# A decoder layer on one core: the opening's bias row, weight split and value products are reordered, and the last expert's scatter and stores are done another way

## The chip, the cores and the metric

The kernel runs on one core of one Trainium2 chip, in one launch. The time is device microseconds. The kernel before takes 456.51 us, the median of 3 runs (455.92 to 458.48). The engines have the names of the profile: PE (TensorE matmul) and PEld (its weight loads), DVE (VectorE), ACT (ScalarE), POOL (GpSimd), SP (SyncE, which here only issues DMAs). A name with a q behind it (DVEq, SPq) is that engine's sequencer, the part that fetches instructions, waits on semaphores and hands work to the engine.

## The reference

The input is x of 4 x 128 x 512 and a context of 4 x 2048 x 512 with a bias and a mask for each key. Cut to what matters:

```python
x = x + cross_attention(layernorm(x), ctx, key_bias, mask)   # 16 heads of 32
x = x + self_attention(layernorm(x))                         # 16 heads of 32, clamped
x = x + experts(layernorm(x))                                # 8 experts, 32 rows of each batch

# cross attention
q = tgt @ Wq.T + bq;  k, v = split(ctx @ Wkv.T + bkv)
attn = softmax(q @ (k / sqrt(32)).T + key_bias + pad)
out = attn @ v @ Wout.T + bout

# experts
g, m = top_k(softmax(x @ gate), 32)
h = gelu(x[m] @ w1) @ w2
out = zeros.at[m].add(g * h).astype(bfloat16)
```

The sum of the experts is rounded to bfloat16 and then added to x in fp32.

## The kernel before, in words

The kernel writes out one instruction list for each engine by hand, and semaphores tie the lists together. So the order of the work is the order of the calls in the source, engine by engine. An engine's sequencer takes its list in order. It stops at an instruction whose semaphore is not there yet, and otherwise hands instructions on while the engine is still busy with earlier ones.

Most products are made in three passes: a tensor is split into a rounded part (`*_hi`, made by ACT) and the rest (`*_lo`, made by DVE), and hi x hi, hi x lo and lo x hi are summed in PSUM as fp32r. The scores and the key projection use plain fp32 instead, which the trace shows as two matmul records for each matmul in the source.

**Opening.** SP queues the loads of x, the key weight `wk`, the first context chunk, the query weight `wq`, the value weight `wv`, the self-value weight `sv` and the output weight `wo` (L292 to L297). ACT issues the output bias row `bo_b` by itself (L547), between two of its own casts. PE turns the normed x, projects the keys of the first chunk (`k_block`, L1286), reads two words of a table into registers (`last_chunk`, L269, and `chunk_before_last`, L272), and makes the queries in three rounds of 16 matmuls (`query_terms`, L1440), one for each pair of parts. DVE adds the bias to x (L853), evacuates the keys (L847), makes the low parts of the query weight (L830), of the value weight and of the self-value weight (both L791), and then evacuates the queries (`queries`, L865 and L866). Then it reads the same two words and a third one (L264), and waits for the scores.

**Context chunks.** Only chunks of 128 keys that hold a valid key are visited, 11 here. Chunk t's scores are made by `scores(t)` (L1383 the key bias, L1388 the products). DVE takes the maxima (L892), ACT the exponents (L486), PE turns the probabilities (L1395), DVE copies three of the four banks (L914) and ACT the fourth (L501). PE's `scores(t + 1)` may start only after these four copies, since it writes the same banks. Between these steps PE projects the next chunk's keys (L1286) and values (`v_project`, L1296, four k steps of three matmuls each). In chunk 0 DVE also makes the low part of `wo` in four pieces (`output_split`, L946).

**The end.** After self attention and the routing, the eight experts follow. The last expert's output is made in two halves of 256 columns, `last_out(half, q)`. `last_half` on DVE multiplies a half by its gate (L1254) into `y_s`; ACT rounds it to `y_hi` (L743), DVE makes `y_lo` (L1256), and PE's `last_scatter` adds both to the sum with a 0/1 matrix `back_now` (L1732, L1733). It has one matmul for each batch and part, on a strip of 32 rows of its own. ACT rounds each batch's sum (L746), POOL (half 0) or DVE (half 1, L1267) adds it to x, and SP stores it (L357), eight stores of 128 KB.

## Time and profile before

| | before |
|---|---|
| median of 3 runs | 456.51 us (455.92 to 458.48) |
| the profiled execution's own time | 456.3 us |
| its span, first to last instruction | 454.6 us |
| PE busy | 437.3 us, 96% of the span |
| DVE busy | 367.7 us, 81% |
| ACT busy | 302.4 us, 67% |
| POOL busy | 87.0 us, 19% |
| mean granted clock of PE | 0.994 of full speed |
| mean DMA rate | 180 GB/s |

All times below count from the span's start. PE is busy nearly the whole time, so a change pays where PE waits, or where work behind PE's last matmul gets shorter. Durations of neighbouring instructions overlap a little: four copies of 0.68 us each may start 0.60 us apart. What an instruction costs a full engine is then the distance of the starts.

### The profile page before, as it was taken

The page shows a single profiled execution, that of the slowest core. Times are in us where ns is not written, and L with a number is a line of the kernel's source. Part 1 is how long each engine was busy: PE and PEld are TensorE (multiplying, and loading weights), DVE is VectorE, ACT ScalarE, POOL GpSimd, SP SyncE. Part 2 cuts the span into 40 slices and gives each one's busy share as a digit, 9 for nine tenths or more (in the row PEclk, how much of TensorE's full clock was granted, in tenths as well). Part 3 has the DMA queues.
Part 4 walks back from the last instruction along what each step waited for, and adds up shares of the span by engine and source line. Part 5 has one row for each costly group of instructions (what it writes and reads, how often), then busy time and mean ns, then how long its engine had stood idle before and what let it go on. Part 6 is the DMA issues. An engine that isn't in the chain of part 4 may idle for free.

```text
span 454.6 us, 9856 instructions
## 1 busy us (share of the span) xinstructions
PE 437.3 (96%) x3424; PEld 363.6 (80%) x3424; DVE 367.7 (81%) x516; ACT 302.4 (67%) x623; POOL 87.0 (19%) x111
## 2 busy tenths in 40 slices
PE   8899999999998999999998999999999999999994
PEld 3778888888886779878887787878788787878793
DVE  6888777777778876668888989888989898998862
ACT  4637666666665643667274878778777778787752
POOL 7100000000000122000043240505050321405002
PEclk9999999999999999999989999999999999999999
DMA  8971000000010922700000599999999999897002
GB/s 287 386 263 26 25 23 23 23 23 23 23 26 10 335 85 82 249 32 3 1 0 1 186 387 385 386 386 387 384 323 358 330 331 358 309 370 291 0 1 92
DMA packets 43105, 82.02 MB, mean 180 GB/s; under 512 B 2632, under 2 KB 3784, under 8 KB 43080
## 3 DMA queue, kind: packets, MB, share of 16 engines
q1 hardware_dynamic: 41960, 81.09, 49.6%
q10 hardware_dynamic: 1120, 0.59, 0.5%
q8 instruction: 16, 0.26, 0.2%
q14 instruction: 9, 0.07, 0.0%
HBM read 80.57 MB, written 1.10 MB: 180 GB/s over the span
## 4 chain that ended last, share of the span: by engine, by line
PE 85%; DVE 6%; DMA 4%; ACT 2%; issue 2%; SPq 1%; DVEq 0%; POOL 0%
PE po L1676 18%; PE pk L1676 11%; PE pv L1676 10%; PE pk L1286 8%; PE pv L1296 6%; PE ps L1315 5%; DMA att_w<-in_sv 4%; PE ps L1395 3%; PE pv L1315 3%; PE po L1702 3%; PE ps L1388 2%; PE po L1408 2%; PE po L1315 2%; PE pk L1315 1%; PE ps L1721 1%
## 5 line engine op out<-in xcount | busy, mean ns | idle before, releaser
L1224 DVE TENSOR_TENSOR w_lo<-att_w,w_hi 128x2048 fp32r<-128x2048 f32 x60 | 138.0, 2309 | 21.2 <-ACT w_hi L704 21.2
L704 ACT CAST w_hi<-att_w 128x2048 fp32r<-128x2048 f32 x60 | 115.1, 1918 | 15.5 <-PE po L1676 15.5
L486 ACT ACTIVATE big_a<-ps,negm 128x128 f32<-128x128 f32 x176 | 62.2, 396 | 0.0
L1676 PE MATMUL po<-w_hi,ht_hi 128*128 128x512 f32 (+1 forms) x128 | 50.0, 391 | 0.0
L1676 PE MATMUL po<-w_hi,ht_lo 128*128 128x512 f32 (+1 forms) x128 | 48.7, 380 | 0.0
L1676 PE MATMUL po<-w_lo,ht_hi 128*128 128x512 f32 (+1 forms) x128 | 48.6, 380 | 0.0
L1286 PE MATMUL pk<-ctx_s,att_w 128*128 128x128 f32 x352 | 42.1, 278 | 0.9 <-DMA ctx_s<-in_ctx_t 0.9
L1286 PEld LDWEIGHTS pk<-ctx_s,att_w 128*128 128x128 f32 x352 | 40.2, 192 | 2.8 <-issue 1.8
L486 ACT ACTIVATION_READ_ACCUMULATOR big_a<-ps,negm 128x1 f32 x176 | 41.5, 236 | 0.0
L892 DVE TENSOR_REDUCE mc<-ps 128x8 f32<-128x1024 f32 x22 | 26.9, 1221 | 11.4 <-PE ps L1388 11.3
L1676 PEld LDWEIGHTS po<-w_hi,ht_lo 128*128 128x128 f32 x128 | 24.0, 188 | 5.1
L423 POOL COPY q_now<-qk 128x512 f32 x10 | 6.2, 615 | 113.0 <-PE ps L1388 113.0
L1676 PEld LDWEIGHTS po<-w_lo,ht_hi 128*128 128x128 f32 x128 | 24.1, 188 | 4.4
L1676 PEld LDWEIGHTS po<-w_hi,ht_hi 128*128 128x128 f32 x128 | 24.0, 188 | 4.4
L454 POOL CAST back_now<-state 128x128 fp32r (+1 forms) x8 | 8.6, 1070 | 94.4 <-PE ps L1721 87.5
L1676 PE MATMUL pk<-w_hi,xin_hi 128*128 128x512 f32 x64 | 26.2, 409 | 0.0
L1676 PE MATMUL pv<-w_hi,xin_hi 128*128 128x512 f32 x64 | 25.9, 405 | 0.0
L1676 PE MATMUL pk<-w_hi,xin_lo 128*128 128x512 f32 x64 | 25.3, 395 | 0.0
L1676 PE MATMUL pk<-w_lo,xin_hi 128*128 128x512 f32 x64 | 25.2, 394 | 0.0
L1676 PE MATMUL pv<-w_lo,xin_hi 128*128 128x512 f32 x64 | 25.2, 394 | 0.0
L1676 PE MATMUL pv<-w_hi,xin_lo 128*128 128x512 f32 x64 | 25.2, 394 | 0.0
L1395 PEld LDWEIGHTS ps<-ident,big_a 128*128 128x128 f32 x176 | 21.2, 140 | 4.3
(346 smaller groups left out, 1022.9 us busy)
## 6 DMA issues: line engine op xcount, KB each, us to landing
att_w<-in_w SPq DMA_DIRECT2D x64, 1024.0 KB, 6.9
ctx_s<-in_ctx_t SPq DMA_DIRECT2D x11, 256.0 KB, 2.6
x_s<-in_x SPq DMA_DIRECT2D x4, 256.0 KB, 3.5
att_w<-in_wk SPq DMA_DIRECT2D x1, 1024.0 KB, 8.1
att_w<-in_wq SPq DMA_DIRECT2D x1, 1024.0 KB, 11.3
att_w<-in_wv SPq DMA_DIRECT2D x1, 1024.0 KB, 13.5
att_w<-in_sv SPq DMA_DIRECT2D x1, 1024.0 KB, 16.2
att_w<-in_wo SPq DMA_DIRECT2D x1, 1024.0 KB, 17.2
```

The source lines that it names most:

```text
L486: ins = a.activation(big_a[:, h], ps[:, c, g * P:(g + 1) * P], ACT.Exp, bias=negm[:, h:h + 1], accum_out=sums[:, h:h + 1])
L704: a.copy(w_hi[:, i % SLOTS], att_w[:, i]).then_inc(hi_ok, 1)
L892: v.tensor_reduce(mc[:, hs], ps[:, 2 * half:2 * half + 2].rearrange("p c (g k) -> p (c g) k", k=P), AX.X, ALU.max).then_inc(loop_dve, 1)
L1224: v.tensor_tensor(w_lo[:, i % SLOTS], att_w[:, i], w_hi[:, i % SLOTS], ALU.subtract).then_inc(lo_ok, 1)
L1286: ins = mm(pk[:, g * P:(g + 1) * P], wk_s[:, k, g * P:(g + 1) * P], ctx_s[:, k], start=k == 0, stop=k == KC - 1)
L1296: ins = mm(pv[:], c[:, k], w[:, 1, k], start=k == 0 and c is ctx_hi and w is w_hi, stop=k == KC - 1 and c is ctx_lo, skip_group_check=True)
L1315: ins = mm(dst, l, r, start=n == 0, stop=n == len(pairs) - 1, skip_group_check=True)
L1388: ins = mm(ps[:, c, g * P:(g + 1) * P], q_now[r, g], kt_s[r, g], start=False, stop=True, skip_group_check=True)
L1395: ins = nc.tensor.transpose(ps[:, c, g * P:(g + 1) * P], big_a[:, c * KC + g], ident[:])
L1408: ins = mm(po[c * DH:(c + 1) * DH, 0, g * P:(g + 1) * P], v_s[:, 0, h, 0:DH], big_b[:, h], start=True, stop=True, skip_group_check=True)
L1676: ins = mm(dst, l, r, start=start and i == 0, stop=i == len(terms) - 1, skip_group_check=True)
L1702: ins = nc.tensor.transpose(po[:, 1, c * P:(c + 1) * P], h_s[:, q % 2, c * P:(c + 1) * P], ident[:])
```

## The change

Five places change; nothing else does.

1. The load of `bo_b` is issued by SP behind `wq` and ahead of `wv`, and no more by ACT.
2. DVE evacuates the first keys and splits the query weight first, and adds the bias row to x after that.
3. The self-value weight's low part is no longer made in one piece ahead of the queries. It is made in two pieces of two k steps: one right after the queries, one in chunk 0 between the maxima and the evacuation of the next keys. The pieces of `wo` stay where they were.
4. PE makes two of the first chunk's four value steps ahead of `scores(0)`, and two behind, instead of one and three.
5. In the last half of the last expert, `y_s` is scattered as it is in plain fp32 with the fp32 matrix `back`, without `y_hi` and `y_lo`. Of the last four stores SP issues batches 0 and 2, and ACT batches 1 and 3.

The core of the diff:

```diff
@@ sync
             sp.dma_start(wq_s, wq.rearrange("(k p) n -> p k n", p=P)).then_inc(in_wq, 16)
+            sp.dma_start(bo_b[:], bo.partition_broadcast(P)).then_inc(in_bo, 16)
...
+            for b in range(B):
+                sp.wait_ge(res_pool, b + 1)
+                sp.dma_start(out[b][:, 0:HALF], x_s[:, b, 0:HALF]).then_inc(stored, 16)
+            for n in (0, 2):
+                sp.wait_ge(res_ok, n + 1)
+                sp.dma_start(out[n][:, HALF:D], x_s[:, n, HALF:D]).then_inc(stored, 16)
@@ scalar
             normed_first(2)
-            act.dma_start(bo_b[:], bo.partition_broadcast(P)).then_inc(in_bo, 16)
...
+            def last_halves():
+                act.wait_ge(y_ok, E)
+                act.wait_ge(sc_mm, E - 1)
+                a.copy(y_hi[:, 0:HALF], y_s[:, 0:HALF]).then_inc(y_hi_ok, 1)
+                for b in range(B):
+                    rounding(0, b)
+                for b in range(B):
+                    rounding(1, b)
+                for n in (1, 3):
+                    act.wait_ge(res_ok, n + 1)
+                    act.dma_start(out[n][:, HALF:D], x_s[:, n, HALF:D]).then_inc(stored, 16)
@@ vector
             split_chunk(0)
+            dve.wait_ge(in_cols, 16)
+            k_evacuate(0)
+            query_split(0)
+            query_split(1)
             dve.wait_ge(in_bo, 16)
             for b in range(B):
                 ins = v.tensor_tensor(x_s[:, b], x_s[:, b], bo_b[:], ALU.add)
             link(ins)
-            dve.wait_ge(in_cols, 16)
-            k_evacuate(0)
-            query_split(0)
-            query_split(1)
             split_att(0)
-            split_att(1)
...
+            def part_split(n, first, end):
+                w, slot, _ = SPLITS[n]
+                dve.wait_ge(att_hi_ok, n + 1)
+                ins = v.tensor_tensor(w_lo[:, slot, first:end], w[:, first:end], w_hi[:, slot, first:end], ALU.subtract)
+                if end == KC:
+                    ins.then_inc(att_lo_ok, 1)
+
+            part_split(1, 0, 2)
...
                 moved_maxima(t, nm)
+                if before is None:
+                    part_split(1, 2, 4)
                 k_evacuate(t + 1)
...
                 v.tensor_scalar(y_s[:, cols], (po[:, 0], pk)[half][:, 0:HALF], gcol[:, E - 1:E], None, ALU.mult).then_inc(y_ok, 1)
+                if half:
+                    return
@@ tensor
             v_project(0, 0)
+            v_project(0, 1)
             pe.wait_ge(q_first, 4)
             pe.wait_ge(q_out, 4)
             scores(0)
-            for k in range(1, KC):
+            for k in range(2, KC):
                 v_project(0, k)
...
             def last_scatter(half):
                 cols = slice(half * HALF, (half + 1) * HALF)
+                if half:
+                    pe.wait_ge(y_ok, E + 1)
+                    pe.wait_ge(rounded_ok, B)
+                    for b in range(B):
+                        r = slice(b * CAP, (b + 1) * CAP)
+                        mm(ps[:, b, cols], back[r, E - 1], y_s[r, cols], start=False, stop=False, skip_group_check=True).then_inc(summed_up, 1)
+                    return
```

DVE's list in the opening, from the first chunk's low part to the table reads, before the change. L842 is the chunk's low part, L853 the bias adds, L847 the keys, L830 the query weight's low part, L791 the value and self-value weights', L865 and L866 the queries, L269 a table read:

```order
L842 TENSOR_TENSOR w_lo<-ctx_s,w_hi 128x4x128
L853 TENSOR_TENSOR x_s<-x_s,bo_b 128x512 x4
L847 TENSOR_TENSOR kt_s<-pk,cols 128x512
L830 TENSOR_TENSOR w_lo<-att_w,w_hi 128x4x256 x2
L791 TENSOR_TENSOR w_lo<-att_w,w_hi 128x2048 x2
L865 TENSOR_SCALAR q_now<-ps,cols 128x128
L866 TENSOR_SCALAR qk<-ps,cols 128x4x128
```

The same piece of DVE's list after the change (line numbers moved by a few: L849 is L842, L854 is L847, L837 is L830, L864 is L853, L798 is L791, L871 and L872 are L865 and L866):

```order
L849 TENSOR_TENSOR w_lo<-ctx_s,w_hi 128x4x128
L854 TENSOR_TENSOR kt_s<-pk,cols 128x512
L837 TENSOR_TENSOR w_lo<-att_w,w_hi 128x4x256 x2
L864 TENSOR_TENSOR x_s<-x_s,bo_b 128x512 x4
L798 TENSOR_TENSOR w_lo<-att_w,w_hi 128x2048
L871 TENSOR_SCALAR q_now<-ps,cols 128x128
L872 TENSOR_SCALAR qk<-ps,cols 128x4x128
```

The four adds stand two splits later, and one of the two weight splits ahead of the queries is gone. Where it went, after the last query and in chunk 0 (L884 is the new split, L908 the maximum, L911 its negation, L916 and L918 the moved maxima, L854 the next keys):

```order
L872 TENSOR_SCALAR qk<-ps,cols 128x4x128
L884 TENSOR_TENSOR w_lo<-att_w,w_hi 128x1024
L269 TENSOR_LOAD table
...
L908 TENSOR_REDUCE mc<-ps 128x8
...
L918 TENSOR_TENSOR neg_max<-neg_max,negm 128x16
L884 TENSOR_TENSOR w_lo<-att_w,w_hi 128x1024
L854 TENSOR_TENSOR kt_s<-pk,cols 128x512
```

One half stands between the queries and the table reads, so the reads are further back in the list; the other half stands ahead of the next keys.

PE's list around the first scores, before (L1440 the queries' third round, L1296 one value step in three matmuls, L1383 and L1388 the scores):

```order
L1440 MATMUL ps<-tr_hi,w_lo 128x512 x16
L1296 MATMUL pv<-w_hi 128x512
L1296 MATMUL pv<-w_lo,w_hi 128x512
L1296 MATMUL pv<-w_hi,w_lo 128x512
L1383 MATMUL ps<-bias,ones 128x512 x4
L1388 MATMUL ps<-kt_s,q_now 128x128 x16
```

and after (L1452, L1308, L1395 and L1400 are the same lines):

```order
L1452 MATMUL ps<-tr_hi,w_lo 128x512 x16
L1308 MATMUL pv<-w_hi 128x512
L1308 MATMUL pv<-w_lo,w_hi 128x512
L1308 MATMUL pv<-w_hi,w_lo 128x512
L1308 MATMUL pv<-w_hi 128x512
L1308 MATMUL pv<-w_lo,w_hi 128x512
L1308 MATMUL pv<-w_hi,w_lo 128x512
L1395 MATMUL ps<-bias,ones 128x512 x4
L1400 MATMUL ps<-kt_s,q_now 128x128 x16
```

Three value matmuls moved from behind the scores to ahead of them. At the end of PE's list the eight fp32r matmuls of the second scatter (L1732 and L1733, four each) become these four:

```order
L1744 MATMUL ps<-y_s,state 128x256 x4
```

The matrix is read from `state`, where `back` lives, and no longer from `back_now`.

## Rows read from the trace of the kernel before

**Rows 1.** The page's busy times, with the share of the span.

```profile
PE 437.3 (96%) x3424; PEld 363.6 (80%) x3424; DVE 367.7 (81%) x516; ACT 302.4 (67%) x623; POOL 87.0 (19%) x111
```

**Rows 2.** Chain that ended last, 0 to 42 us: start us, us, what.

```profile
23.24 2.29 DVE w_lo L791
...
28.54 0.67 DVE qk L866
```

**Rows 3.** Timeline of PE: start us, us, engine line op out<-in xcount [idle before <-releaser].

```profile
16.39 3.97 PE L1440 MATMUL ps<-tr_hi,w_hi 128*128 128x512 f32 x16 [0.80 <-ACT w_hi L516]
...
23.94 3.89 PE L1440 MATMUL ps<-tr_hi,w_lo 128*128 128x512 f32 x16
...
28.14 0.39 PE L1296 MATMUL pv<-w_hi,w_lo 128*128 128x512 f32 x1
29.30 0.40 PE L1383 MATMUL ps<-bias,ones 32*128 32x512 bf16 x4 [0.78 <-DVE qk L866]
...
41.13 0.40 PE L1383 MATMUL ps<-bias,ones 32*128 32x512 bf16 x4 [0.16 <-issue]
```

**Rows 4.** Timeline of ACT and its queue in the opening and chunk 0.

```profile
8.41 0.33 ACTq L547 DMA_DIRECT2D bo_b<-in_bo  x1
...
15.20 1.04 ACT L516 CAST w_hi<-att_w 128x1024 fp32r<-128x1024 f32 x1 [1.95 <-DMA att_w<-in_wq]
...
40.31 0.59 ACT L501 COPY big_b<-ps 128x512 f32<-128x512 f32 x1 [1.04 <-PE ps L1395]
```

**Rows 5.** Timeline of the end, from the last half's gate on.

```profile
447.87 0.48 DVE L1254 TENSOR_SCALAR y_s<-pk,gcol 128x256 f32<-128x256 f32 x1 [3.47 <-PE pk L1676]
...
449.64 0.40 PE L1732 MATMUL ps<-y_hi,back_now 32*128 32x256 f32 x4 [1.81 <-issue]
...
450.14 1.20 ACT L746 CAST rounded<-ps 128x256 bf16<-128x256 f32 x4 [1.35 <-PE ps L1733]
450.55 1.43 DVE L1267 TENSOR_TENSOR x_s<-x_s,rounded 128x256 f32<-128x256 f32 x4 [1.01 <-ACT rounded L746]
```

**Rows 6.** The last two stores by line (ns, first and last start us), and landing.

```profile
L357 SPq DMA_DIRECT2D out<-x_s x2: 448/449/450, 451.9 to 452.4; - x2
...
DMA to landing us min/median/max: 1.8/1.8/1.8
```

**Rows 7.** The bias row's DMA: KB, and us from issue to landing.

```profile
bo_b<-in_bo ACTq DMA_DIRECT2D x1, 256.0 KB, 5.8
```

**Rows 8.** DMA queues in 11.7 to 12.7 us: packets, MB, share of 16 engines.

```profile
q1 hardware_dynamic: 137, 0.27, 70.6%
q10 hardware_dynamic: 66, 0.14, 35.9%
```

**Rows 9.** Sequencers' table reads by line: durations ns, first and last start us.

```profile
L272 PEldq SEQ_ASSERT  x1: 18/18/18, 15.9 to 15.9; - x1
...
L269 DVEq TENSOR_LOAD <-table x1: 550/550/550, 27.9 to 27.9; - x1
...
L264 DVEq SEQ_ASSERT  x1: 23/23/23, 30.4 to 30.4; - x1
```

**Rows 10.** Timeline of DVE in the opening and chunk 0.

```profile
14.94 2.48 DVE L853 TENSOR_TENSOR x_s<-x_s,bo_b 128x512 f32<-128x512 f32 x4
...
18.06 2.35 DVE L830 TENSOR_TENSOR w_lo<-att_w,w_hi 128x1024 fp32r<-128x1024 f32 x2
...
30.65 1.23 DVE L892 TENSOR_REDUCE mc<-ps 128x8 f32<-128x1024 f32 x1 [1.45 <-PE ps L1388]
...
36.46 0.69 DVE L847 TENSOR_TENSOR kt_s<-pk,cols 128x512 f32<-128x512 f32 x1 [1.32 <-PE pk L1286]
...
40.10 0.68 DVE L914 COPY big_b<-ps 128x512 f32<-128x512 f32 x1
```

**Rows 11.** The first scores' matmuls by line: durations ns, first and last start us.

```profile
L1388 PE MATMUL ps<-kt_s,q_now x32: 265/270/270, 29.5 to 30.3; 32*128 32x128 f32 x32
```

More of the change, by code:

```diff
@@ L352, in _ @@
                     sp.dma_start(att_w[:, i], w_tile(e, i)).then_inc(raw_in[i], 16)
-            for half in range(2):
-                cols = slice(half * HALF, (half + 1) * HALF)
-                for b in range(B):
-                    sp.wait_ge((res_pool, res_ok)[half], b + 1)
-                    sp.dma_start(out[b][:, cols], x_s[:, b, cols]).then_inc(stored, 16)
+            for b in range(B):
[4 more added lines that the diff above has]
+                sp.dma_start(out[n][:, HALF:D], x_s[:, n, HALF:D]).then_inc(stored, 16)
             sp.wait_ge(stored, 32 * B)
@@ L736, in expert, with rounding @@
                 a.copy(y_hi[:], y_s[:]).then_inc(y_hi_ok, 1)
-            def last_half(half):
+            def rounding(half, b):
                 cols = slice(half * HALF, (half + 1) * HALF)
-                act.wait_ge(y_ok, E + half)
-                if half == 0:
-                    act.wait_ge(sc_mm, E - 1)
-                a.copy(y_hi[:, cols], y_s[:, cols]).then_inc(y_hi_ok, 1)
-                for b in range(B):
-                    act.wait_ge(summed_up, half * B + b + 1)
-                    a.copy(rounded[:, b, cols], ps[:, b, cols]).then_inc(rounded_ok, 1)
+                act.wait_ge(summed_up, half * B + b + 1)
+                a.copy(rounded[:, b, cols], ps[:, b, cols]).then_inc(rounded_ok, 1)
+            def last_halves():
+                act.wait_ge(y_ok, E)
+                act.wait_ge(sc_mm, E - 1)
+                a.copy(y_hi[:, 0:HALF], y_s[:, 0:HALF]).then_inc(y_hi_ok, 1)
+                for b in range(B):
+                    rounding(0, b)
[4 more added lines that the diff above has]
+                    act.dma_start(out[n][:, HALF:D], x_s[:, n, HALF:D]).then_inc(stored, 16)
             expert(0, True)
@@ L751, in _ @@
             expert(E - 1, False)
-            last_half(0)
-            last_half(1)
+            last_halves()
         @block.vector
@@ L940, in attended @@
                 v.tensor_tensor(natural(norm[:, b]), natural(state[:, b]), by_head(norm_c[:, b]), ALU.mult).then_inc(normed[1], 1)
-            def output_split(k):
-                w, slot, _ = SPLITS[2]
-                dve.wait_ge(att_hi_ok, 3)
-                ins = v.tensor_tensor(w_lo[:, slot, k], w[:, k], w_hi[:, slot, k], ALU.subtract)
-                if k == KC - 1:
-                    ins.then_inc(att_lo_ok, 1)
             def chunk(t, before, at_end=False):
@@ L962, in chunk @@
                 else:
-                    output_split(0)
+                    part_split(2, 0, 1)
                 turned_probs(t, 0)
                 if before is None:
-                    output_split(1)
+                    part_split(2, 1, 2)
                 if at_end:
@@ L981, in _ @@
             chunk(0, None)
-            output_split(2)
-            output_split(3)
+            part_split(2, 2, 3)
+            part_split(2, 3, 4)
             with dve.Fori(1, prev) as t:
@@ L1725, in last_scatter @@
                 cols = slice(half * HALF, (half + 1) * HALF)
+                if half:
[5 more added lines that the diff above has]
+                    return
                 pe.wait_ge(back_staged, E)
-                pe.wait_ge(y_lo_ok, E + half)
-                if half:
-                    pe.wait_ge(rounded_ok, B)
+                pe.wait_ge(y_lo_ok, E)
                 for b in range(B):
```

## The prediction

> **What bounds the kernel now.** I read the busy times first: PE works 96% of the span [rows 1]. So the change can pay only where PE waits at the opening, or behind PE's last weight product. The chain of waits comes next. In the opening it runs through the self-value weight: its low part on DVE from 23.24, the queries behind it up to 28.54 + 0.67 = 29.21, and then the first scores [rows 2]. PE's own timeline shows the price: the third value matmul starts at 28.14, and PE could go on 0.23 later, at 28.37. The scores start at 29.30 [rows 3]. That is 0.93 us lost, 0.78 of it shown as idle for the queries. Further back PE waits 0.80 us for the rounded query weight [rows 3], whose cast starts when its load lands, at 15.2 [rows 4]. At the end the stretch behind the last product is serial: gate at 447.87, scatter at 449.64, rounding at 450.14, add at 450.55 [rows 5], last store issued at 452.4 and landed 1.8 later [rows 6].
>
> **Query weight sooner (part 1).** `bo_b` is 256 KB. ACT issues it at 8.41 [rows 4] and it lands 5.8 later [rows 7], at 14.2, ahead of the query weight's 15.2 [rows 4]. In 11.7 to 12.7, when the query weight is arriving, ACT's queue q10 moves 0.14 MB beside 0.27 MB on q1 [rows 8]. All of the bias row thus comes out of the query weight's time: 0.26 MB at the 0.41 MB per us of that window is 0.64 us. Behind it in one queue, the row no longer does this: the weight lands near 14.55, its first half is rounded by 15.6, and PE could start at 15.7 in place of 16.39. But PE also reads its two table words, and the last step of that stands at 15.9 whatever the weight does (it waits for the table, not for the weight) [rows 9]. So PE starts the queries at about 16.05: **0.35 us**, with 0 (the row never was in the way) and 0.67 (the reads don't bind) as ends. `wv`, `sv` and `wo` have the same bytes ahead of them as before.
>
> **DVE's new order (part 2).** The adds of 2.48 us [rows 10] move from ahead of the keys to behind the query weight. Keys, query weight, adds and value weight (0.6 + 2.3 + 2.5 + 2.3) from 15.65 on end at about 23.3. The first query is complete on PE one quarter into the third round, 23.94 + 0.97 = 24.9 less 0.35. So DVE waits for PE there by 1.2 us, and the order costs nothing. The cover is gone only if the bias row lands after about 19.8.
>
> **The self-value split and the value step (parts 3, 4).** Without the second 2.3 us split, each query is evacuated as PE finishes it. PE's last round ends at 27.83 - 0.35 = 27.5, DVE's last query about 1.0 later, 28.5. Two value steps keep PE busy until 28.37 + 0.70 - 0.35 = 28.7, so the first scores start at about 28.75 in place of 29.30 and end at 30.05 in place of 30.59. PE's hole is full, and PE reaches the next keys 1.2 us sooner. What is late next is DVE. Its maximum started at 30.65, right behind the scores [rows 10], but its three table reads had ended only at 30.4 [rows 9]. They began at 27.9, which is when PE's last query came (27.83): DVE's sequencer hangs on that query's semaphore and then runs ahead of its engine. From 27.9 to 30.45 they take 2.6 us. After the change they begin at 27.55 + 0.05, end at 30.2, and the maximum starts at 30.25: **0.40 us** earlier, not 0.55. This needs the sequencer to pass the new half split while two queries are still queued ahead of it. The first read's 27.9 [rows 9] against the last query's start at 28.5 [rows 2] shows it two instructions ahead, not three.
>
> The Trainium skill ("Advanced Engine Details and Errata", section Engine Queue Depths) gives VectorE a queue of 8. By that rule the reads start at once, as I take it; if two were the limit, they would wait for the half split to move up, the case of the first rival.
>
> The first half split, (2.35)/2, about 1.15 us [rows 10], lies between 28.5 and 30.25, and is free. The second lies in the 1.32 us in which DVE waited for the keys [rows 10]. PE now brings these keys early enough, so the wait becomes work and about 0.2 us are left over. DVE is full from there to its third copy, which ended at 40.10 + 0.68 = 40.78 [rows 10]. It now ends 0.40 + 0.20 sooner, 40.2. The second scores stood at 41.13 [rows 3], 0.35 behind that copy, since ACT's copy ended at 40.31 + 0.59 = 40.90 [rows 4]. ACT's chain moves by over 1 us, so some 0.15 of this goes too. I take **0.75 us** for the whole opening. From the second scores on PE runs with hardly a gap, and what it gains there is kept. The ends are -0.15 (the reads wait for the half split) and 1.35 (no table read binds, neither on PE nor on DVE).
>
> **The end (part 5).** Before, PE starts 449.64; now it needs only the gated half, 447.87 + 0.48 = 448.35, and PE starts 0.1 later, at 448.45: 1.19 us sooner. The fp32 scatter is dearer. The first scores are fp32 on the same four strips of 32 rows: 32 records of 128 columns start within 0.8 us [rows 11], 0.028 apart, so the strips run side by side, and each strip takes 0.11 a record. For 256 columns that is 0.22 a record, two records for each batch, and then 0.27 + 0.11 until the second is through: the first batch is ready 0.61 after the start. Before it took 450.14 - 449.64 = 0.50 to ACT's reaction, and would take 0.64 now. So ACT starts at 449.1, **1.05 us** sooner. The ends are 0.5 (strips one after another: the fourth batch comes at 8 x 0.22 + 0.16, 0.55 later than ACT would take it) and 1.2. POOL's adds of half 0 are not on this path. Then the stores: DVE's fourth add ended at 450.55 + 1.43 = 451.98 and the last store was issued at 452.4 [rows 5, 6], because the issues, the last two of 0.45 each, queued on SP. With two on each sequencer the last is issued right behind its add: **0.3 us**, ends 0 and 0.35, landing unchanged. Together 1.35.
>
> On the stores a page of the Trainium skill speaks against hoping for more: "Trainium Kernel Development and Optimization", Key Constraints, says that all queues share the same 16 DMA engines, so that issuing from several saves only issue time. That is the 0.3 above.
>
> **The sum.** 0.75 + 1.35 = 2.1 us. The profiled execution took 456.3 (span 454.6, the other 1.7 unchanged) and would take 454.2. It lies 0.2 under the median of 456.5, so I predict 454.4. A measurement of this kernel can tell about 0.5%, 2.3 us, from no change; the forecast lies just inside this, and its own range is 453.9 to 454.9.
>
> **Rivals.**
> - *The opening gives nothing.* DVE's reads wait until the half split starts (28.4 and not 27.6), the maximum then starts near 31.0, 0.4 later than before. The filled gap gives 0.2 back. Or the query weight is no earlier, since another load takes the bytes. For it: the reads are the last to end already now, 0.2 before the maximum. Against: the sequencer did pass two. Total gain 1.2 to 1.6, 455.1.
> - *The reads don't bind.* They begin 0.6 earlier, or overlap better, and the opening gives what the load and PE's hole offer, 1.35. Total 2.7, 453.8. Against it: both sequencers' reads stand within 0.2 us of what follows them.
> - *The strips are serial in fp32* in the scatter. Total 1.5 to 1.6, 455.0. Against: the 0.028 us spacing [rows 11].
> - *Slower: ACT's stores land late.* The large load from ACT's queue took 5.8 us to land [rows 7], SP's stores 1.8 [rows 6]. If a store from ACT took what its load did, the last would land 4.0 later, and the time would be 456.5 - 2.1 + 4.0 = 458.4. It decides from a landing of 3.9 us on. Against: in the 5.8 us the DMA engines were full with SP's weights; at the end they are empty.
>
> **Chances.** Forecast 0.47, nothing from the opening 0.24, reads don't bind 0.17, serial strips 0.08, slower 0.04 (that the edits don't act as written: none left over, since the order lists show each). Faster by over 0.5% means under 454.2: the 0.17 and somewhat under half of the forecast's 0.47, 0.38 in all. Slower 0.04. Same 0.58. The range runs from the second rival's 453.8 less 0.4 to the first's 455.1 plus 0.7.
>
> **What would show it.** Right: q1 alone active until the query weight has landed near 14.6; PE's queries at 16.05; the first scores at 28.75 with no idle before them; DVE's maximum at 30.2 to 30.3 with the reads just ended; the second scores near 40.35. At the end: PE's scatter 0.58 behind the gate's start, ACT 0.65 behind that, the last store issued within 0.1 of the last add. Wrong: a maximum at or after 30.65, a query start still at 16.4, an ACT store that lands later than SP's, or a gain that is given back in a later chunk.

## Result: 453.72 us against 456.51, and the profile after

| | before | changed |
|---|---|---|
| median (lowest to highest), us | 456.51 (455.92 to 459.11), 7 runs | 453.72 (452.63 to 455.0), 7 runs |
| ratio, 95% interval | | 0.9925 (0.9901 to 0.9948) |
| profiled execution, us (span) | 456.3 (454.6) | 455.0 (453.3) |

The kernel is 0.75% faster. Timed twice more, each time beside the kernel before on one chip, the changed kernel gave 0.9946 (0.993 to 0.9962) and 0.9959 (0.9945 to 0.9973), that is 2.3 and 2.0 us instead of 2.8. The time lies inside the whole range of the prediction (453.4 to 455.8), but 0.7 us under the predicted 454.4 and just outside the 453.9 to 454.9 that the forecast claimed for itself. It is nearest to the second rival's 453.8. "No change beyond 0.5%" was held likelier (0.58) than a faster kernel (0.38), and the first interval lies wholly beyond 0.5%; those of the two repeats reach across it.

The two profiled executions differ by only 1.3 us. Three differences make this up, each read from TensorE's (PE's) and VectorE's (DVE's) timelines:

| stretch, us | before | changed | difference |
|---|---|---|---|
| start to second scores | 41.13 | 39.95 | -1.18 |
| second scores to first expert product | 206.11 | 207.32 | +1.21 |
| first expert product to last half's gate | 200.63 | 200.62 | 0 |
| gate to the end | 6.72 | 5.40 | -1.32 |

**The opening.** PE's timeline of the changed kernel, in the columns of [rows 3]:

```profile
15.77 3.96 PE L1452 MATMUL ps<-tr_hi,w_hi 128*128 128x512 f32 x16 [0.18 <-issue]
...
23.30 3.90 PE L1452 MATMUL ps<-tr_hi,w_lo 128*128 128x512 f32 x16
...
28.17 0.39 PE L1308 MATMUL pv<-w_hi,w_lo 128*128 128x512 f32 x1
28.49 0.40 PE L1395 MATMUL ps<-bias,ones 32*128 32x512 bf16 x4
...
39.95 0.40 PE L1395 MATMUL ps<-bias,ones 32*128 32x512 bf16 x4 [0.47 <-DVE big_b L930]
```

The first scores no longer wait: the value steps end as they start (the 0.78 us of [rows 3] are gone). The query starts 0.62 us sooner, and what released it is no longer ACT's cast but "issue", PE's own sequencer. ACT's timeline shows that the weight was there long before, at 14.20 for 15.20 [rows 4], and the queue of the bias row is now SP's:

```profile
11.33 0.62 ACT L543 CAST w_hi<-ctx_s 128x512 fp32r<-128x512 f32 x1 [0.75 <-DMA ctx_s<-in_ctx_t]
11.86 0.58 ACT L481 CAST tr_hi<-pv 128x512 fp32r<-128x512 f32 x1
12.33 0.59 ACT L481 CAST tr_hi<-ps 128x512 fp32r<-128x512 f32 x1
14.20 1.04 ACT L518 CAST w_hi<-att_w 128x1024 fp32r<-128x1024 f32 x1 [1.28 <-DMA att_w<-in_wq]
```

In 11.7 to 12.7 us one queue is left of the two of [rows 8], and the row now lands 11.7 us after its issue, harmlessly:

```profile
q1 hardware_dynamic: 209, 0.41, 106.2%
```

```profile
bo_b<-in_bo SPq DMA_DIRECT2D x1, 256.0 KB, 11.7
```

The sequencers' reads, answering to [rows 9] (durations in ns, first and last start in us):

```profile
L272 PEldq SEQ_ASSERT  x1: 18/18/18, 15.6 to 15.6; - x1
...
L269 DVEq TENSOR_LOAD <-table x1: 547/547/547, 27.2 to 27.2; - x1
...
L264 DVEq SEQ_ASSERT  x44: 23/23/23, 29.8 to 159.0; - x44
```

PE's reads ended at 15.6, and not at 15.9 as the forecast held fixed. DVE's began at 27.2, while the half split stood at 28.16 in its list; so its sequencer did not wait for the split, which settles the first rival. DVE's timeline, answering to [rows 10]:

```profile
18.57 2.49 DVE L864 TENSOR_TENSOR x_s<-x_s,bo_b 128x512 f32<-128x512 f32 x4
...
24.43 0.35 DVE L871 TENSOR_SCALAR q_now<-ps,cols 128x128 f32<-128x128 f32 x1 [1.04 <-PE ps L1452]
...
28.16 1.22 DVE L884 TENSOR_TENSOR w_lo<-att_w,w_hi 128x1024 fp32r<-128x1024 f32 x1
29.86 1.23 DVE L908 TENSOR_REDUCE mc<-ps 128x8 f32<-128x1024 f32 x1 [0.48 <-PE ps L1400]
...
34.27 1.22 DVE L884 TENSOR_TENSOR w_lo<-att_w,w_hi 128x1024 fp32r<-128x1024 f32 x1
35.40 0.69 DVE L854 TENSOR_TENSOR kt_s<-pk,cols 128x512 f32<-128x512 f32 x1
```

The adds are hidden (DVE still waits 1.04 us for the first query), and the second half split fills what was a wait of 1.32 us for the keys [rows 10]: the keys now follow without a wait.

**The end**, all engines, answering to [rows 5]. The profile shows each fp32 product of the source as two records, so the four are x8 here. The last two rows are the issues of the stores on SP and ACT (start and length of the stretch that holds both):

```profile
447.89 0.48 DVE L1264 TENSOR_SCALAR y_s<-pk,gcol 128x256 f32<-128x256 f32 x1 [3.46 <-PE pk L1689]
...
448.43 0.71 PE L1744 MATMUL ps<-y_s,state 32*128 32x256 f32 x8 [0.58 <-DVE y_s L1264]
449.16 1.20 ACT L742 CAST rounded<-ps 128x256 bf16<-128x256 f32 x4 [1.69 <-PE ps L1744]
449.56 1.43 DVE L1279 TENSOR_TENSOR x_s<-x_s,rounded 128x256 f32<-128x256 f32 x4 [1.19 <-ACT rounded L742]
450.02 1.00 SPq L359 DMA_DIRECT2D out<-x_s  x2
450.36 1.01 ACTq L754 DMA_DIRECT2D out<-x_s  x2
```

The gate stands where it stood, and every later step 1.0 to 1.4 us earlier. ACT's two stores, by line:

```profile
L754 ACTq DMA_DIRECT2D out<-x_s x2: 344/353/362, 450.4 to 451.0; - x2
...
DMA to landing us min/median/max: 1.8/1.8/1.9
```

The last is issued at 451.0 (452.4 in [rows 6]) and lands as fast as one of SP's: the slower rival is out.

**The routing took it back in this one execution.** Stretches of 4 us; the columns are length, PE, PEld, DVE, ACT and POOL busy (with counts), PE's granted clock (1.00 is 2.4 GHz, 0.50 is 1.2 GHz), DMA share, GB/s. Before:

```profile
232.00:236.00 4.00, 4.00 (x24) 3.60 (x24) 3.20 (x18) 3.38 (x7) 1.48 (x4) 0.76 0.00 0
236.00:240.00 4.00, 3.58 (x13) 2.29 (x11) 2.84 (x14) 2.19 (x2) 3.77 (x3) 0.81 0.00 0
240.00:244.00 4.00, 2.63 (x16) 2.11 (x17) 3.15 (x9) 0.44 (x3) 1.47 (x2) 1.00 0.02 4
```

Changed:

```profile
232.00:236.00 4.00, 3.45 (x21) 2.67 (x21) 2.87 (x17) 3.54 (x6) 1.77 (x3) 1.00 0.00 0
236.00:240.00 4.00, 1.90 (x9) 1.27 (x8) 3.69 (x14) 1.00 (x1) 2.73 (x3) 1.00 0.00 0
240.00:244.00 4.00, 3.71 (x17) 3.23 (x17) 2.02 (x6) 0.92 (x3) 2.44 (x2) 0.63 0.02 4
244.00:248.00 4.00, 4.00 (x31) 3.92 (x31) 3.13 (x9) 2.78 (x10) 0.00 (x0) 0.95 0.00 0
```

In both PE's clock is at half for a while. Before, this falls on filling products (`keep_busy`, which only fill PE's idle time; nobody needs their result), and behind them PE still waits 1.50 us for DVE's `kt_s`. In the changed kernel's profiled execution it falls on the 32 gather products, all of which the experts wait for: they take 5.30 us from the first start to the last instead of 3.82.

### The profile page after: what moved, and what is told of

Its sections match the earlier page's. It is cut to its first block, busy times and chain, and to the rows that moved or that the text cites. A ratio compares the mean times of both kernels' runs of the same rounds, so it can differ in the third digit from the quotient of the medians.

```text
span 453.3 us, 9856 instructions
## 1 busy us (share of the span) xinstructions
PE 437.7 (97%) x3424; PEld 363.9 (80%) x3424; DVE 367.4 (81%) x516; ACT 302.1 (67%) x622; POOL 86.9 (19%) x111
## 4 chain that ended last, share of the span: by engine, by line
PE 84%; DVE 9%; ACT 2%; issue 2%; DMA 1%; POOL 1%; DVEq 1%; SPq 0%; POOLq 0%
PE po L1689 18%; PE pk L1689 11%; PE pv L1689 10%; PE pk L1298 8%; PE pv L1308 5%; PE ps L1327 5%; PE po L1715 3%; PE ps L1407 3%; PE pv L1327 3%; PE ps L1452 3%; PE ps L1400 2%; PE po L1420 2%; PE pk L1327 1%; PE po L1327 1%; DMA x_s<-in_x 1%
## 5 line engine op out<-in xcount | busy, mean ns | idle before, releaser
L908 DVE TENSOR_REDUCE mc<-ps 128x8 f32<-128x1024 f32 x22 | 26.9, 1221 | 10.4 <-PE ps L1400 10.3
```

The source lines that it names most:

```text
L908: v.tensor_reduce(mc[:, hs], ps[:, 2 * half:2 * half + 2].rearrange("p c (g k) -> p (c g) k", k=P), AX.X, ALU.max).then_inc(loop_dve, 1)
```

## Experiments

All medians stand beside the kernel before on the same chip. There it took 456.07 (e1 to e4), 456.33 (e7, e8, e10, e12), 456.53 (e6, e9, e11, e14), 455.78 (e15, e16) and 456.51 us (e17, e18). "Reads" are the table reads; "the chunk's cast" is ACT's cast of the first context chunk (L543), which starts when the chunk has landed.

### The two halves of the change

**e1_opening**: the changed kernel with the old end (scatter, rounding and stores; the diff is cut to its core).

```diff
-            last_halves()
+            last_half(0)
+            last_half(1)
...
```

> The changed kernel with the last half's scatter and stores as they were before (y_hi and y_lo, eight matmuls, all stores from SP). Theory (the opening is worth about 1.2 us to the second scores, the end 1.3, and the rest of what single executions differ by is the clock in the routing): second scores start near 39.95 against 41.13 before; from the last half's gate to the end of the span 6.7 us as before; median 1.2 us (0.26%) under the kernel before. Rival (my prediction's sizes, and more than 1.3 from the end): second scores near 40.4, median 0.7 under before.

455.40 us, ratio 0.9989 (0.9977 to 1.0): 0.67 us under before by the medians. The interval reaches 1.0, so the times alone don't tell this gain from none. In its profile the second scores stand at 40.10, near my 39.95, but the median is that of the rival.

**e2_end**: the kernel before with the new end (the same edit the other way round).

> The kernel before with the end of the change alone (fp32 scatter of the last half, last four stores from two queues). Theory: second scores at 41.1 as before; from the last half's gate to the end of the span 5.4 us against 6.7; median 1.3 us (0.28%) under the kernel before. Rival (the medians' 2.8 us come mostly from the end): more than 2 us under before.

454.72 us, ratio 0.9974 (0.9964 to 0.9985): 1.35 us under before; gate to end 5.40 us. So by the medians opening and end add up: 0.67 + 1.35 = 2.0, near the two repeats of the whole change (2.3 and 2.0).

### Parts of the opening

**e3_row**: before, with only the bias row moved behind the query weight. **e4_no_row**: changed, with the row back on ACT.

```diff
             sp.dma_start(wq_s, wq.rearrange("(k p) n -> p k n", p=P)).then_inc(in_wq, 16)
+            sp.dma_start(bo_b[:], bo.partition_broadcast(P)).then_inc(in_bo, 16)
...
-            act.dma_start(bo_b[:], bo.partition_broadcast(P)).then_inc(in_bo, 16)
```

> The kernel before with one edit: SP issues the output bias row behind the query weight, ACT no more. DVE's and PE's lists are as before. Theory: the row took its bytes out of the query weight and of the context chunk ahead of it, so the first cast of the query weight starts about 1 us sooner (14.2 against 15.2), the chunk's cast 0.3 sooner, PE's two table reads end 0.3 sooner (15.6) and the queries start at 15.8. The second scores hardly gain (0 to 0.3 us), since DVE's whole self-value split still ends at 25.5 or so ahead of the queries. Rival (the reads end at 15.9 whatever lands when): queries start at 16.05. Second rival (the row in front of wv delays the self-value weight, and DVE's queries get later): second scores later than 41.2.

> The changed kernel with the output bias row issued by ACT at its old place. Theory: queries on PE start at 16.4 as before, all behind 0.6 later than in the changed kernel, the second scores at 40.5 to 40.6, so the row is worth half of the opening's gain. Rival (DVE bounds chunk 0 whatever PE does, so the row is worth nothing there): second scores at 39.95 as in the changed kernel.

e3 456.27 us, 1.0008 (0.9992 to 1.0025); e4 453.89 us, 0.9947 (0.9929 to 0.9966). The row took what the forecast charged to it: from the chunk's cast to the first cast of the query weight it is 3.3 to 3.5 us in the three profiles with the row on ACT (before, e2, e4) and 2.7 to 2.9 in the twelve with it on SP and that cast at its old place. Yet e4 starts the query only 0.07 later than the changed kernel, measured from the chunk's cast (4.51 for 4.44), and its second scores come only 0.06 later (28.68 for 28.62). e4's query stands 1.19 us behind the weight's cast, as in the kernel before; the changed kernel's stands 1.57 behind, so there something other than the weight holds PE. Of my two expectations for e4 the rival was the nearer. And e3 gains nothing in its time: its first scores start 13.11 us behind the query's start, 12.91 before. What is late there is the self-value split, which still stands ahead of DVE's queries and waits for its weight's cast:

```profile
22.65 2.29 DVE L791 TENSOR_TENSOR w_lo<-att_w,w_hi 128x2048 fp32r<-128x2048 f32 x1 [0.39 <-ACT w_hi L476]
```

**e7_split_whole**: changed, with the self-value split in one piece ahead of the queries again. **e8_value_behind**: changed, with the second value step behind the scores again.

```diff
             split_att(0)
+            split_att(1)
...
-            part_split(1, 0, 2)
...
-                if before is None:
-                    part_split(1, 2, 4)
```

```diff
             v_project(0, 0)
-            v_project(0, 1)
...
-            for k in range(2, KC):
+            for k in range(1, KC):
```

> The changed kernel with the self-value split back in one piece ahead of the queries; two value steps still stand ahead of the first scores. Theory (this split is what held the queries): the first scores start at about 29.3, their maximum at 30.65, the second scores at 40.7 to 41.0, so 0.8 to 1.0 us behind the changed kernel there. Rival (the earlier query weight and the value step are the gain): second scores at 39.9 to 40.2.

> The changed kernel with the second value step back behind the first scores. Theory (DVE bounds chunk 0, and it waits first for the first scores): the scores start 0.3 us sooner than in the changed kernel, at 28.2 to 28.3, DVE's maximum stays near 29.8 since its table reads end there, and the second scores stand at 39.9 as in the changed kernel: the value step moved ahead is worth nothing. Rival (PE bounds chunk 0): second scores 0.3 us later or more.

e7 454.49 us, 0.997 (0.9951 to 0.9989); e8 453.91 us, 0.9951 (0.9933 to 0.9968). My expectation for e7 was too large. Its first scores come 0.54 later against the query's start (13.26 us for 12.72), but from the maximum to the second scores it then needs 9.70 us where the changed kernel needs 10.09. DVE does the same work on either side of the maximum, and only 0.13 us are left at the second scores, measured from the chunk's cast (28.75 for 28.62). e7's median stands 0.6 us above e8's of the same comparison; the two intervals overlap, so the times don't settle it. e8's second scores come 0.12 later; its time is that of the changed kernel. The same stretch lies between 28.58 and 28.73 in the eight profiles with the changed opening as it is, so 0.06, 0.13 and 0.12 are hardly more than their scatter. Taken out one by one, row, split and value step thus cost 0.31 us together, where the whole opening gave 0.6 to 0.8. The new place of the bias adds (part 2) was not taken out alone, so what the rest hangs on is not shown.

### What holds the query's start

In all 14 profiles with ACT's casts and PE's reads in their old order, the reads end 4.24 to 4.27 us behind the chunk's cast, wherever that lies (10.83 to 11.71 us). ACT's rows above show why: the casts of turned batches 2 and 3 stand behind the chunk's cast on ACT's list, DVE's remainders of them ahead of the table on DVE's, and the table ahead of the reads.

**e14_cast_later** (run again as **e17_cast_again** beside **e18_changed_again**, the changed kernel itself):

```diff
             transposed(0, 1)
-            split_chunk(0)
             transposed(0, 2)
             transposed(0, 3)
+            split_chunk(0)
```

> The changed kernel with ScalarE's cast of the first context chunk moved behind the casts of the last two turned self-state batches. In nine profiles so far TensorE's table reads ended 4.24 to 4.27 us after that cast began, and the query's first product began 0.16 us after the reads. Theory A (the reads are late because the table stands on VectorE behind the splits of batches 2 and 3, whose casts stand behind the chunk's landing on ScalarE): the reads end 0.4 to 1.0 us sooner against the chunk's cast (less than 3.9 us after the chunk's cast would have begun), and the query starts only 0.2 to 0.4 us sooner, since its weight's cast is next. Rival B (the reads are bound by something else of the opening, such as the key's products ahead of them on TensorE's list): the reads end as before against the landing and the query's start moves later by 0 to 0.3 us, for the chunk's cast comes later. Median by A 453.3 to 453.9, by B 453.7 to 454.2.

**e6_pe_reads_late**: changed, PE's reads behind the first scores and value steps. The wait for the table itself (`table_ok`) stays ahead of the queries.

```diff
-            last = last_chunk(pe)
-            prev = chunk_before_last(pe)
...
+            pe.wait_ge(table_ok, 3)
...
             for k in range(2, KC):
                 v_project(0, k)
+            last = last_chunk(pe)
+            prev = chunk_before_last(pe)
```

> The changed kernel with TensorE's two table reads moved from ahead of the query projection to behind the first batch's scores and value steps. Theory A (the reads bind the query's start in the changed kernel): the first query product no longer stands 0.16 us behind a read but starts when its rounded weight is there, 0.2 to 0.9 us sooner against the chunk's cast (4.4 us after it in the changed kernel, 3.5 to 4.2 here), while the reads cost about their own 0.7 to 1.0 us later only if TensorE doesn't wait there anyway. Rival B (the weight's cast or the turned remainders bind just as well): the start moves by less than 0.1 us. In both cases VectorE's own reads still stand ahead of its first maximum, so the second scores come at most 0.3 us sooner: median 453.4 to 454.0.

e14: 452.97 us, 0.9934 (0.9914 to 0.9953). Its reads and the start of its query, from the rows of line 272 and PE's timeline:

```profile
L272 PEldq SEQ_ASSERT  x1: 18/18/18, 14.6 to 14.6; - x1
```

```profile
15.20 1.17 PE L1452 MATMUL ps<-tr_hi,w_hi 128*128 128x512 f32 x4
```

The chunk's cast now waits for the two ahead of it and not for the landing, so it is no mark here; the query weight's first cast is one (14.01, and 14.20 in the changed kernel). The reads end 0.56 us behind that cast for 1.40, and the query starts 1.19 behind it for 1.57, as in the kernel before (16.39 - 15.20 = 1.19): it is bound by the weight again. That the reads end so much sooner with one cast moved shows the chain.

e6: 453.86 us, 0.9935 (0.991 to 0.996); the query starts at 14.92, 1.27 us behind its weight's cast, and 0.03 behind the start of the last key product (14.89), so here PE is simply full. Its reads, now beside DVE's maximum, cost nothing: from the chunk's cast to the second scores it is 28.19 us for 28.62, so the gain at the query's start is kept. With both, the rival that something other than the table's reads holds the changed kernel's query falls.

> The version with ScalarE's cast of the first chunk behind the casts of the turned batches once more, on one chip with the changed kernel. Theory A (the table's reads bound the changed kernel's query start by 0.35 to 0.4 us and the second scores by as much): the median stands 0.4 to 0.8 us below the changed kernel's of this same comparison, and the second scores come 28.0 to 28.1 us behind the chunk's landing or 0.5 us sooner than in the changed kernel. Rival B (what is gained in the opening is lost in the scatter between executions, since landings and the place of the half clock move the time by 0.5 to 1.5 us): the two medians lie within 0.3 us of each other.

> The changed kernel word for word, as the other side of that comparison: 453.4 to 454.2 us median. A third profiled execution of it: by the theory that the place and length of TensorE's half clock belong to the execution, its routing (second scores to first expert product) is either 205.8 to 206.1 us or 206.6 to 207.8 us, and its time goes with it; the query's first product stands 0.16 to 0.18 us behind TensorE's last table read in any case.

On one chip: e17 453.71 us, 0.9944 (0.9928 to 0.996); e18, the changed kernel, 454.50 us, 0.9959 (0.9945 to 0.9973). The later cast is 0.8 us better by the medians. By the profiles its query starts 1.19 us behind the weight's cast for 1.72, and its second scores come 0.9 us sooner (0.23 of it because the weight came sooner too). The two intervals overlap, so by time alone it isn't settled; the profiles agree in both pairs, with 0.4 to 0.5 us at the query's start. e14's median is the lowest of the study, but its ratio is not clear of the changed kernel's. The changed kernel's own median here is above the 453.4 to 454.2 that I expected.

### What holds DVE's first maximum

**e16_both**: e14, and DVE's two reads ahead of its four query steps (e14's edit is left out of the diff).

```diff
+            last = last_chunk(dve)
+            prev = chunk_before_last(dve)
             queries(0)
...
             part_split(1, 0, 2)
-            last = last_chunk(dve)
-            prev = chunk_before_last(dve)
```

> The changed kernel with two edits together, as a version that may beat both: ScalarE's cast of the first chunk behind the casts of the turned batches (452.97 us median by itself), and VectorE's two table reads moved from behind its four query steps to ahead of them, where it waits for TensorE's first query sum (1.04 us in the changed kernel, 0.81 with the cast moved). Theory A (VectorE's reads, which end 0.04 us ahead of its first maximum, bind that maximum): the maximum begins sooner against the first scores, 1.0 to 1.25 us behind their start where it is 1.38 now, and everything behind comes 0.1 to 0.4 us sooner; median 452.5 to 452.9. Rival B (the scores and the batch's sum bind it as well, and the reads that stood beside the queries' arithmetic now push those later, since 2.6 us of reads don't fit into a wait of 0.8 us where the list stands still): the first query step comes 0.5 to 1.8 us later, the first scores with it, median 453.5 to 454.8.

453.44 us, 0.9947 (0.9928 to 0.9966): no better than e14. DVE's last read now begins at 27.0 and ends at 27.57, 2.05 us ahead of the maximum:

```profile
L264 DVEq TENSOR_LOAD <-table x44: 301/304/320, 27.0 to 158.1; - x44
```

```profile
29.62 1.22 DVE L909 TENSOR_REDUCE mc<-ps 128x8 f32<-128x1024 f32 x1 [0.50 <-PE ps L1401]
```

Still the maximum starts 1.36 us behind the first scores (28.26), as in every kernel of the study but e8 (1.35 to 1.38, while the reads ended 0.04 to 2.05 us ahead of it). The scores bind it, too. That the reads end 0.04 us before it in the changed kernel is a near tie. In e8, whose scores start sooner behind the query (12.59 us for 12.72), the reads do bind: the maximum starts 1.50 us behind the scores and 0.05 behind the reads. Neither side of my expectation came true: nothing gained, nothing lost.

### The stores

**e9_stores_sp**: changed, all four last stores on SP.

```diff
-            for n in (0, 2):
+            for n in range(B):
...
-                for n in (1, 3):
-                    act.wait_ge(res_ok, n + 1)
-                    act.dma_start(out[n][:, HALF:D], x_s[:, n, HALF:D]).then_inc(stored, 16)
```

> The changed kernel with all four of the last stores issued by SyncE, none by ScalarE. The profile of the changed kernel has SyncE's issues 0.67 us apart (450.02 and 450.69) and ScalarE's at 450.36 and 451.03. Theory A (two issuers relieve SyncE's list by what was forecast, 0.3 us): with four issues on one list the last one comes 0.2 to 0.6 us later and the stretch from the last gate product to the end goes from 5.40 to 5.6 to 6.0 us. Rival B (the issues are not the bound, the sums that come 0.33 us apart are): the stretch stays within 0.1 us of 5.40. Median by A 453.9 to 454.4, by B 453.5 to 453.9.

453.87 us, 0.9949 (0.993 to 0.9968), within the scatter; the profile tells more:

```profile
L359 SPq DMA_DIRECT2D out<-x_s x4: 333/437/445, 449.9 to 451.2; - x4
```

With four on one list an issue takes 0.44 us (median) instead of 0.33, while DVE's adds, which they wait for, start 0.33 to 0.35 apart. Gate to end is 5.69 us for 5.40: the second issuer is worth 0.29 us.

### The half clock in the routing

**e12_busy2**, **e11_busy14**, **e10_busy18**: the changed kernel with 2, 14 or 18 filling products ahead of the slots' transposes instead of 10. **e15_again**: the changed kernel word for word.

```diff
-            keep_busy(10, 7)
+            keep_busy(14, 7)
```

> The changed kernel with 2 and not 10 of the idle-filling matmuls ahead of the slots' transpose. Theory: PE is idle for longer ahead of the gathers, the clock is at half in them more often and perhaps for longer: 5.3 us for the gathers in the profile, and a median 0.5 to 1.5 us over the changed kernel's. Rival: no difference.

> The changed kernel with 14 filling products ahead of the slots' transposes instead of 10. TensorE's granted clock was at half once in the routing of every kernel profiled, in the gathers (at 241 to 242 us, 5.3 us for the gathers) or ahead of them (at 232 to 235 us, gathers 3.8 us). Theory A (where the half clock falls is the chip's, not set by these products): the executions fall into two groups 1.2 to 1.5 us apart as they do for the changed kernel, median 453.5 to 454.3, and the profile shows either place. Rival B (more filling keeps the clock up through the gathers): no execution in the upper group, gathers 3.8 us, median 453.2 to 453.7.

> The changed kernel with 18 and not 10 of the idle-filling matmuls ahead of the slots' transpose in the routing. Theory (in some executions PE's clock falls to half while the gathers run, since PE was idle for 2 us just ahead, and this costs about 1.5 us): with the hole filled the gathers run at full clock in every execution, 3.8 us from first to last record against 5.3, the runs of one kernel spread less, and the median is 0.3 to 1 us under the changed kernel's. If the clock falls earlier, among the filling matmuls, the longer row of them delays the transpose by up to 1.5 us instead. Rival (the clock in the routing is no matter of the matmuls there, or the spread has another source): median and spread as in the changed kernel, 453.7, 452.6 to 455.0.

> The changed kernel once more, word for word, for a second profiled execution of the same program beside the first (455.0 us, gathers at half clock, 5.30 us, first expert product 207.32 us behind the second scores). Theory A (where TensorE's half clock falls differs from one execution of one kernel to the next and makes the two groups of times): the profiled execution lies either near 453.7 with gathers of 3.8 us and 205.8 to 206.1 us from the second scores to the first expert product, or near 455.0 with 5.3 and 207.3; a time of 453.4 to 453.9 together with gathers of 5.3 us, or of 455 together with gathers of 3.8 us, would speak against it. Rival B (the place of the half clock belongs to the program's own arrangement): the profile shows gathers of 5.3 us again whatever its time is. Median 453.4 to 454.3 by both.

| kernel | median, us | profiled, us | where at half clock, from | gathers, us | second scores to experts, us |
|---|---|---|---|---|---|
| changed | 453.72 | 455.0 | gathers, 241.0 | 5.30 | 207.32 |
| e15 | 453.47 | 454.55 | ahead, long, 231.3 | 3.82 | 207.21 |
| e18 | 454.50 | 454.93 | ahead, long, 232.5 | 3.80 | 206.83 |
| e12 (2) | 455.09 | 454.35 | ahead and into the gathers, longest, 233.3 | 4.95 | 207.16 |
| e11 (14) | 454.25 | 455.14 | gathers, 241.8 | 5.31 | 207.35 |
| e10 (18) | 453.60 | 455.05 | ahead, long, 231.8 | 3.82 | 207.78 |
| e14 | 452.97 | 452.93 | ahead, short, 232.6 | 3.81 | 205.79 |

The stretches of e15 (first) and e14 (second), in the columns given above:

```profile
228.00:232.00 4.00, 4.00 (x36) 3.97 (x34) 3.72 (x14) 3.19 (x7) 0.74 (x3) 0.91 0.00 0
232.00:236.00 4.00, 4.00 (x14) 3.32 (x14) 1.85 (x11) 2.70 (x6) 1.20 (x3) 0.50 0.00 0
236.00:240.00 4.00, 3.59 (x12) 2.52 (x10) 3.12 (x15) 1.55 (x1) 3.30 (x3) 0.74 0.00 0
240.00:244.00 4.00, 3.06 (x20) 2.54 (x21) 3.01 (x8) 0.87 (x4) 1.89 (x2) 1.00 0.02 4
```

```profile
228.00:232.00 4.00, 4.00 (x39) 3.97 (x37) 3.72 (x16) 3.40 (x7) 0.95 (x3) 1.00 0.00 0
232.00:236.00 4.00, 4.00 (x14) 2.96 (x14) 2.63 (x15) 3.53 (x6) 2.15 (x4) 0.58 0.00 0
236.00:240.00 4.00, 2.76 (x12) 1.74 (x10) 3.69 (x15) 0.40 (x1) 2.13 (x2) 0.99 0.00 0
```

The same program fell to half clock in the gathers once and ahead of them twice, so the place belongs to the execution. That refutes the reading that the change pushed the gathers into half clock. But the other theory's simple link (gathers at full clock, so a time near 453.7) failed too: e15's profiled 454.55 had gathers of 3.82 us and, ahead of them, 6.8 us at half clock where e14 had 3.4. In all 18 profiles the same holds: with one short stretch ahead of the gathers the routing takes 205.8 to 206.2 us, with a long one or with one in the gathers 206.6 to 207.8. The runs of some kernels fall apart by as much: those of e14 into seven at 452.8 to 453.1 and two at 454.5 to 454.6. Those of e11 and e18 spread without such a gap, and the runs without a profile show only a mean clock, so that the half clock makes the groups is likely, not shown. More filling products (14, 18) buy nothing that can be told from the changed kernel. With 2 the median is 1.5 us above that of 18 beside it (455.09 and 453.60), and the clock stayed at half longest. What sets the place isn't settled.

## Why the prediction was near, and where it failed

**The end: right.** Forecast 1.35 us, measured 1.32 in the profile and 1.35 in e2's median (ratio 0.9974, so 0.7 to 1.6 us by its interval). Term by term: PE's scatter at 448.43 for a forecast 448.45; ACT at 449.16 for 449.1 (strips side by side, 8 records in 0.71 us: the serial rival is out); the issuers 0.29 (e9) for 0.3. ACT's stores landed like SP's.

**The opening: the mechanisms mostly right, the start mis-sized.** Forecast 0.75 us at the second scores, measured 1.18 in the profile. The step that failed is "the last step of that stands at 15.9 whatever the weight does (it waits for the table, not for the weight)". True, it waits for the table. But the table waits, over DVE and ACT, for the landing of the first context chunk, and that came 0.34 us sooner. So the query started 0.62 sooner and not 0.35. Of the 0.43 us by which the opening beat its forecast in this profile, 0.27 are this step, and 0.12 more came by the maximum.

Whether the bias row had held up the chunk is not shown. The chunk's cast starts at 11.54 to 11.71 in the three profiles with the row on ACT and at 10.83 to 11.65, 11.25 on average, in the twelve with it on SP where the cast waits for the landing. But e3, whose profile has the chunk's cast at 11.20 and the second scores at 40.45, gained nothing in its median, and its interval leaves at most 0.4 us. So the earlier landing may be luck of the profiled execution.

With the landing taken off, the size was right: measured from the chunk's cast, the opening gave 29.46 - 28.62 = 0.84 us, or 0.62 with e2 (29.24), whose opening is that of before: on both sides of the 0.75. The e1 median says 0.67. The part behind the maximum was right as well: from there to the second scores 10.48 us became 10.09, 0.39 for a forecast 0.35. The row's own 0.35 was too much: with e4 it is 0.07 at the query's start and 0.06 at the second scores, since PE's reads hold the query once the weight is early. The forecast had a reading wrong here. "Both sequencers' reads stand within 0.2 us of what follows them" was so on DVE (0.19), but PE's reads ended at 15.92, 0.47 ahead of the query's 16.39.

**The maximum: right for a wrong reason.** "DVE's three table reads bind it, 0.40, not 0.55" gave 30.25; it came at 29.86. With the 0.27 of the query's start taken off, 0.12 are left. The reads did begin with PE's last query (27.2), with three instructions of the engine still ahead of them, so two are not the limit. The Trainium skill's queue of 8 (Advanced Engine Details and Errata, section Engine Queue Depths) fits this; no run here fills the queue beyond three. But e16 shows that the scores bind just as well. So the rival "the reads don't bind" was half right on DVE: they tie with the scores, and taking them away alone (e16) gave nothing. On PE they did bind, by 0.4 to 0.5 us, which e14 and e6 took away. That the first median, 453.72, lies at this rival's 453.8 is chance: its opening of 1.35 needed both reads not to bind.

**The sum.** Forecast 2.1 us. Measured 2.8, 2.3 and 2.0 in three comparisons, and 2.0 as the sum of the two halves. The size was right within the scatter between comparisons; the first happened to lie at its upper end. What was off is the weight of "same": a gain of 2.1 was set against a bound of 2.3 us, which is nearly an even chance and was given 0.38. The forecast also took no account of the half clock: its place and length made routings of 205.8 to 207.8 us in the profiles, and the changed kernel's profiled executions lie 0.4 to 1.3 us above their medians.

## What to carry to other kernels

Follow a wait that "stands whatever else does" one engine further: here a table of two words on one engine's list hung, through in-order lists of two others, on a load that had nothing to do with it, and moving one cast by two places took 0.4 to 0.5 us off the query's start, more than the 0.35 forecast for the bias row, the edit that was meant for it. Where an edit moves work from one side of a serial point to the other on the same full engine (the split of e7), count both sides before you book the gain. And compare a profiled execution with its kernel's median before you explain a difference between two profiles by the change.

## What was not expected of the hardware

- The granted clock of one and the same program fell to 1.2 GHz at 231.3, at 232.5 or at 241.0 us in three executions. It did so both in a full stretch (PE busy 4.00 of 4 us around e15's fall at 231.3) and behind a thin one (1.90 of 4 us ahead of the first changed profile's). In the gathers it cost 1.5 us (5.30 for 3.82).
- A store issue took 0.33 us on SP with two of them (0.34 to 0.36 on ACT) and up to 0.45 with four in a row; the landing, 1.7 to 1.8 us from SP and 1.8 to 1.9 from ACT, hardly depended on the issuing engine.
